# A two-layer decoder on one core: inside a step of the second cross attention, maximum products before score products

## The chip, the cores and the metric

The kernel runs on one core of one Trainium2 chip. The metric is the device time of one execution in microseconds; the time before is the median of three runs. A separate profiled execution gives the rows that are shown here. The engines are called as the profile calls them: PE (TensorE matmul) and PEld (its weight loads), DVE (VectorE), ACT (ScalarE), POOL (GpSimd), and SP, which only issues DMAs.

## The reference, cut to what matters

A decoder of two layers works on 16 batches of 56 tokens and 128 channels. Each layer is a self attention, a cross attention to a context of 1500 positions, and a feed-forward part with experts. The change touches the second layer's cross attention, with 16 heads of 8 channels:

```
def _L1_xattn_ref(q, k, v, W_q, b_q, W_k, b_k, W_v, b_v, W_o, b_o):
    qh = _split_heads(q @ W_q.T + b_q, bs)
    kh = _split_heads(k @ W_k.T + b_k, bs)
    vh = _split_heads(v @ W_v.T + b_v, bs)
    scores = jnp.einsum('bhqd,bhkd->bhqk', qh, kh) / jnp.sqrt(jnp.float32(D_K))
    weight = jax.nn.softmax(scores, axis=-1)
    attn = jnp.einsum('bhqk,bhkd->bhqd', weight, vh)
    concat = attn.transpose(0, 2, 1, 3).reshape(bs, -1, D_MODEL)
    return concat @ W_o.T + b_o
...
x = x + _L1_xattn_ref(_layernorm(x, axis=-1), ctx_1024, ctx_1024, ...)
```

Here q is the normalised token block and k and v are both the context.

## The kernel before

The kernel is written by hand for each engine, with semaphores between them; each engine runs its instructions in the order of the program. The second cross attention is the group of functions whose names begin with `late_`: `late_tensor` (PE), `late_scalar` (ACT), `late_vector` (DVE), `late_gpsimd` (POOL), `late_sync` (SP).

The softmax is done in two passes over the same score matrix. First the row maxima of a batch are found: PE makes a product of queries and keys of 112 rows by 500 columns (`maxima`, L1083), DVE reduces it to one column (L1405), 24 times for a batch. Then the negative maxima are turned by PE (`turn_maxima`, L1091), copied by ACT (L1333), and stored as two more rows of the query tile, a high part and a low part, by two small DMAs that ACT issues (`send_maxima`, L1344). The low part is made by DVE (`low_maxima`, L1420) after DVE's two reductions of that step. With those rows in place a second product gives scores that are already lowered by the maximum (`scores`, L1103: four matmuls, two for each half), ACT takes their exponential straight from PSUM (`exps`, L1324), PE multiplies the result with the values (`product`, L1117: eight matmuls in groups of 32 columns), and POOL adds the exponentials up over the chunks (`add`, L1232) for the row sums, which PE spreads (`sums`, L1125) and DVE inverts (`normalise`). For the last batch DVE does the adding (`last_add`).

The main loop of `rest()` on PE has one step for each chunk c of 125 context positions, 12 steps to a batch, counted by g. In a step with c = g mod 12 of batch b = g div 12, PE does several things that belong to different batches:

- the scores of chunk g - 4 (so that scores lag the maxima by 16 steps);
- two maximum products of batch b + 1;
- in steps c = 2, 3 and 4 a third of the key projection of batch b + 2 (`project`, `keys`, L1042), and in steps c = 6, 8 and 10 a third of its value projection (L1048). All of them use PSUM bank 7, so a third of the keys waits until ACT (L1293, high part) and DVE (L1399, low part) have taken the third before;
- in step c = 0 the turning of the maxima of batch b;
- the product with the values of chunk g - 5;
- in one step of a batch the sums of the batch before.

ACT's loop does in each step the two exponentials first, then the evacuation of the projections, the masked queries of batch b + 2 in step 5 (`queries`, L1311), and the two small DMAs of the maxima in steps 0 and 1. ACT's second small DMA waits for `low_maxima`, and whatever ACT has to do in step 2 stands behind it. DVE's loop does in each step the two reductions and then the rest.

The keys reach the stacked key tile `late_k` by 12 DMAs of 187.5 KB for a batch, issued by SP (`stack`, L1275) as soon as the low part of the last third is ready; the first maximum product of that batch (`maxima` with u = 0, at c = 0) waits for all of them (`m["stack"]`). Maximum products use PSUM banks 0, 1 and 2 in turn, so one waits for the reduction of the third before it (`m["mx"]`). Scores have two banks and wait for the exponential of the same half one step earlier; the exponentials go around five buffers (`LATE_P`).

The lines of the wait for the stack are these:

```
def maxima(b, u):
    ...
    if u == 0:
        pe.wait_ge(m["stack"], 16 * 12 * (b + 1))
```

Of the kernel before, what the change touches and what calls it, by code (L numbers as in the profile page):

```python
# [23 lines left out]
B, S, D = 16, 56, 128  # L24
# [45 lines left out]
def decoder_kernel(nc, t, out):  # L70
# [4 lines left out]
    with ctx:  # L75
# [959 lines left out]
        def late_tensor(pe):  # L1035
            m = la

            def keys(b, piece, bank):

                if piece == 0:  # L1040
                    pe.wait_ge(ld_late[b % 2], 16 * (b // 2 + 1))
                nc.tensor.matmul(PS[:, bank, 0:KB], xa_w[:, 1, :], late_ctx[b % 2][:, piece * KB:(piece + 1) * KB],  # L1042
                                 start=True, stop=True).then_inc(m["kmm"], 1)

            def values(b, piece, bank):
                for j in range(4):
                    c = 4 * piece + j
                    mm = nc.tensor.matmul(PS[0:KC, bank, j * 128:(j + 1) * 128],  # L1048
                                          late_ctx[b % 2][:, c * KC:(c + 1) * KC], xa_w[:, 2, :],
                                          start=True, stop=True)  # L1050
                mm.then_inc(m["vmm"], 1)

            def project(b, piece):

                if piece == 0:
                    if b >= 2:
                        pe.wait_ge(m["nmlow"], b - 1)
                elif piece < 4:
                    pe.wait_ge(m["khi"], 3 * b + piece)
                    pe.wait_ge(m["klo"], 3 * b + piece)  # L1060
                else:
                    pe.wait_ge(m["vev"], 3 * b + piece - 3)
                if piece < 3:
                    keys(b, piece, 7)
                else:
                    values(b, piece - 3, 7)

            def maxima(b, u):

                s, w = u // NKB, u % NKB  # L1070
                if u == 0:
                    pe.wait_ge(m["stack"], 16 * 12 * (b + 1))
                    if b:
                        pe.wait_ge(m["qset"], b)
                if b == 0:
                    if u < NKB:
                        pe.wait_ge(m["qlo"], u + 1)
                    if u % (2 * NKB) == 0:
                        pe.wait_ge(m["q0set"], u // (2 * NKB) + 1)
                if b or s:  # L1080
                    pe.wait_ge(m["mx"], NKB * (8 * b + s - 1) + w + 1)
                at = (s // 2) * S2 + w * KB
                nc.tensor.matmul(PS[0:2 * S, w, 0:KB], late_q[b % 3][0:3 * QUAD, s * 2 * S:(s + 1) * 2 * S],  # L1083
                                 late_k[b % 3][0:3 * QUAD, at:at + KB], start=True, stop=True)\
                    .then_inc(m["mxmm"], 1)

            def turn_maxima(b):

                pe.wait_ge(m["nmsplit"], b + 1)
                pe.wait_ge(m["vev"], 3 * min(b + 2, B))  # L1090
                nc.tensor.transpose(PS[0:8, 7, 0:2 * S], late_nm[b % 2],  # L1091
                                    ident[0:2 * S, 0:2 * S]).then_inc(m["nmtr"], 1)

            def scores(b, c, half):
                at = 2 * (NC * b + c) + half
                if c == 0 and half == 0:
                    pe.wait_ge(m["nmrow"], 2 * 16 * (b + 1))
                if at >= 2:
                    pe.wait_ge(m["exp"], at - 1)
                for a in range(2):  # L1100
                    j = 2 * half + a
                    first = min(j * 4 * S, HQ - SCOLS)
                    mm = nc.tensor.matmul(PS[0:KC, 3 + half, a * SCOLS:(a + 1) * SCOLS],  # L1103
                                          late_k[b % 3][:, j * S2 + c * KC:j * S2 + (c + 1) * KC],
                                          late_q[b % 3][:, first:first + SCOLS], start=True, stop=True)
                mm.then_inc(m["sc"], 1)

            def product(b, c):
                n = NC * b + c
                if c == 0:  # L1110
                    if b >= 2:
                        pe.wait_ge(m["norm"], b - 1)
                    pe.wait_ge(m["vev"], 3 * b + 3)
                pe.wait_ge(m["exp"], 2 * n + 2)
                for j in range(4):
                    r = slice(32 * j, 32 * j + 32)
                    mm = nc.tensor.matmul(PS[r, 5 + b % 2, 0:4 * S], late_v[b % 3][0:KC, c, r],  # L1117
                                          late_p[n % LATE_P][:, j * 4 * S:(j + 1) * 4 * S],
                                          start=c == 0, stop=c == NC - 1)
                mm.then_inc(m["pv"], 1)  # L1120

            def sums(b):
                pe.wait_ge(m["padd"], (NC - 1) * (b + 1))
                for j in range(4):
                    mm = nc.tensor.matmul(PS[32 * j:32 * j + 32, 5 + b % 2, 4 * S:8 * S], ones[0:KC, 0:32],  # L1125
                                          late_acc[b % 2][:, j * 4 * S:(j + 1) * 4 * S], start=True, stop=True)
                mm.then_inc(m["sum"], 1)
# [27 lines left out]
            def rest():  # L1155
                def project_queries(j, a, bank):
                    nc.tensor.matmul(PS[0:3 * QUAD, bank, 0:HALF],
                                     late_wq[:, j, :, :].rearrange("p r c -> p (r c)"),
                                     XN[:, a * HALF:(a + 1) * HALF], start=True, stop=True).then_inc(m["qp"], 1)

                pe.wait_ge(xn_ready, 2 * 4 + 2)
                pe.wait_ge(m["wqrep"], 1)
                for j in range(4):
                    project_queries(j, 0, j)
                for c in range(NC):
                    maxima(0, 2 * c)
                    maxima(0, 2 * c + 1)
                    if c < 3:
                        if c == 0:
                            pe.wait_ge(ld_late[1], 16)  # L1170
                        pe.wait_ge(m["vev"], c + 1)
                        keys(1, c, 4 + c)
                    elif c < 7:
                        if c == 4:
                            pe.wait_ge(m["qlo"], 4)
                        if c > 4:
                            pe.wait_ge(m["klo"], 3 + c - 4)
                        project_queries(c - 3, 1, Q_BANKS[c - 3])
                    elif c < 10:
                        if c == 7:  # L1180
                            pe.wait_ge(m["klo"], 6)
                        else:
                            pe.wait_ge(m["qlo"], c - 3)
                        values(1, c - 7, V_BANKS[c - 7])
                pe.wait_ge(m["qlo"], 8)
                for g in range(NC * B + LAG):
                    b, c = g // NC, g % NC
                    n = g - LAG
                    if 0 <= n:
                        scores(n // NC, n % NC, 0)  # L1190
                        scores(n // NC, n % NC, 1)
                    if b + 1 < B:
                        maxima(b + 1, 2 * c)
                        maxima(b + 1, 2 * c + 1)
                    if b + 2 < B and c in (2, 3, 4):
                        project(b + 2, c - 2)
                    if b + 2 < B and c in (6, 8, 10):
                        project(b + 2, c // 2)
                    if c == 0 and 0 <= b < B:
                        turn_maxima(b)  # L1200
                    if 1 <= n:
                        product((n - 1) // NC, (n - 1) % NC)
                    if n >= NC and n % NC == 2:
                        sums(n // NC - 1)
                    if b == B - 1 and c == 5:
                        pe.wait_ge(m["wo"], 1)
                        out_bias(0, HB)
                        out_heads(0, HB, range(4))
                product(B - 1, NC - 1)
                out_bias(HB, B - 1)  # L1210
                out_heads(HB, B - 1, range(1))
                sums(B - 1)
                out_heads(HB, B - 1, range(1, 4))
                out_bias(B - 1, B)
                out_heads(B - 1, B, range(4))
# [997 lines left out]
```

## Time and profile before

| what | value |
| --- | --- |
| time before, median of three runs | 1419.98 us (1418.58 to 1421.03) |
| profiled execution: span from the first to the last instruction | 1421.9 us |
| profiled execution: its own time, apart from the span | not given separately |
| busy share over the span: PE, PEld, DVE, ACT, POOL | 96%, 71%, 73%, 61%, 54% |
| the steps that hold both score and maximum products, in the span | 902.3 us to 1283 us |
| mean granted TensorE clock over the span | 0.976 of full speed |

The span is that of the one profiled execution; the median is that of other executions. A busy PE is not PE at its peak: matmuls are pipelined and their ends are modelled in the records. A wait for several semaphores is put down to the one that came last.

### The profile page before, as it was taken

Reading aid. Unit: us, or ns where it says so; the run is one execution under the profiler, and the core shown is the slowest. Engines: PE = TensorE matmul, PEld = TensorE weight load, DVE = VectorE, ACT = ScalarE, POOL = GpSimd, SP = SyncE. Lnnn points to the kernel's source line nnn. Section 1 sums busy time; section 2 is a strip of 40 time slices with the busy share of each in tenths; the row PEclk is TensorE's granted clock in tenths of the full one; section 3 lists DMA queues with packets and bytes.
Section 4 is the critical chain, followed back from the end, with each engine's and each line's share of the span. In section 5 each row is a group of like instructions: output and inputs, shape, how many; then the busy total and the mean of one; then the engine's idle time right before and its main releaser. Section 6 shows DMA issues by size and latency. Waiting matters only on the chain.

```text
span 1421.9 us, 25408 instructions
## 1 busy us (share of the span) xinstructions
PE 1361.6 (96%) x9220; PEld 1016.4 (71%) x9220; DVE 1039.0 (73%) x2112; ACT 860.5 (61%) x1849; POOL 766.6 (54%) x431
## 2 busy tenths in 40 slices
PE   7889999999999999999998987899999999999998
PEld 4647888888888888888865754556656556555687
DVE  6458778888777877788854677677777777774687
ACT  4537667666667666677632553466666666664665
POOL 5036443334444444432261292488888888894463
PEclk9899999999999999999998999899999999997999
DMA  3132222211122222221150232535536446330131
GB/s 85 59 94 52 57 58 57 52 39 43 48 54 58 56 53 58 57 57 36 40 156 4 66 67 57 139 88 133 129 89 144 119 99 143 87 96 1 58 107 43
DMA packets 71803, 104.39 MB, mean 73 GB/s; under 512 B 14670, under 2 KB 54934, under 8 KB 71550
## 3 DMA queue, kind: packets, MB, share of 16 engines
q1 hardware_dynamic: 60062, 91.39, 25.8%
q10 hardware_dynamic: 11616, 11.38, 2.8%
q8 instruction: 73, 1.20, 0.4%
q14 instruction: 52, 0.43, 0.1%
HBM read 63.65 MB, written 2.11 MB: 46 GB/s over the span
## 4 chain that ended last, share of the span: by engine, by line
PE 77%; DVE 7%; POOL 4%; ACT 3%; DMA 3%; issue 2%; SPq 1%; ACTq 1%; POOLq 0%; DVEq 0%
PE PS L700 10%; PE PS L714 6%; PE PS L1103 6%; PE PS L688 5%; PE PS L716 5%; PE PS L689 5%; PE PS L715 5%; PE PS L690 5%; PE PS L1117 4%; POOL QO_area L1232 4%; PE PS L1083 3%; PE PS L1042 2%; PE PS L1048 2%; PE PS L1776 2%; PE PS L743 2%
## 5 line engine op out<-in xcount | busy, mean ns | idle before, releaser
L1232 POOL TENSOR_TENSOR QO_area<-QO_area,prob_a 125x896 f32<-125x896 f32 x150 | 315.1, 2101 | 22.7 <-ACT prob_a L1324 3.2
L866 ACT ACTIVATE HL<-PS 125x512 fp32r<-125x512 f32 (+1 forms) x384 | 206.5, 538 | 176.5 <-PE PS L700 161.0
L958 DVE TENSOR_TENSOR HL<-PS,HL 125x512 fp32r<-125x512 f32 (+1 forms) x384 | 238.2, 623 | 73.1 <-ACT HL L866 52.4
L1405 DVE TENSOR_REDUCE QO_area<-PS 112x1 f32<-112x500 f32 x384 | 240.6, 672 | 68.0 <-PE PS L1083 67.8
L1324 ACT ACTIVATE prob_a<-PS 125x448 f32<-125x448 f32 x384 | 187.6, 540 | 111.0 <-PE PS L1103 88.7
L773 POOL TENSOR_TENSOR HL<-ctx_area,ones 125x512 fp32r<-125x512 f32 (+1 forms) x64 | 93.0, 1453 | 244.0 <-PE PS L716 193.9
L1103 PEld LDWEIGHTS PS<-HL 98*125 98x125 f32 x768 | 106.3, 193 | 73.8 <-ACT prob_a L1324 44.8
L688 PE MATMUL PS<-HL 128*128 128x500 f32 x336 | 153.0, 455 | 4.8 <-DVE HL L928 3.9
L714 PE MATMUL PS<-HL 125*128 125x512 f32 (+1 forms) x384 | 155.7, 406 | 1.6 <-DVE HL L958 1.4
L876 ACT ACTIVATE prob_a<-prob_a,neg_max 128x500 f32<-128x500 f32 x192 | 135.5, 706 | 26.7 <-DVE neg_max L950 25.4
L1103 PE MATMUL PS<-HL 98*125 98x256 f32 x768 | 148.6, 317 | 0.6 <-ACT prob_a L1324 0.6
L716 PE MATMUL PS<-HL 125*128 125x512 f32 (+1 forms) x384 | 140.4, 366 | 0.0
L715 PE MATMUL PS<-HL 125*128 125x512 f32 (+1 forms) x384 | 140.1, 365 | 0.0
L1083 PE MATMUL PS<-HL 96*112 96x500 f32 x384 | 126.6, 406 | 6.6 <-DVE QO_area L1405 4.2
L689 PE MATMUL PS<-HL 128*128 128x500 f32 x336 | 131.6, 392 | 0.0
L690 PE MATMUL PS<-HL 128*128 128x500 f32 x336 | 131.1, 390 | 0.0
L700 PEld LDWEIGHTS PS<-ident,prob_a 128*125 128x125 f32 x768 | 113.5, 186 | 17.4 <-ACT prob_a L876 0.9
L776 POOL TENSOR_TENSOR HL<-ctx_area,HL 125x512 fp32r<-125x512 f32 (+1 forms) x64 | 116.7, 1823 | 5.0
L700 PE MATMUL PS<-ident,prob_a 128*125 128x128 f32 x768 | 115.4, 272 | 0.5 <-ACT prob_a L876 0.5
L773 POOL TENSOR_TENSOR HL<-QO_area,ones 128x896 fp32r<-128x896 f32 x15 | 25.2, 1681 | 145.3 <-PE PS L690 130.9
L876 ACT ACTIVATE prob_b<-prob_b,neg_max 128x500 f32<-128x500 f32 x144 | 101.8, 707 | 0.0
L942 DVE CUSTOM_DVE_ANT_0 prob_a<-PS,proj_w,head_scale 128x500 f32<-128x500 f32 x128 | 93.5, 731 | 6.1 <-PE PS L690 1.9
(261 smaller groups left out, 2718.9 us busy)
## 6 DMA issues: line engine op xcount, KB each, us to landing
HL<-prob_b SPq DMA_DIRECT2D x128, 187.5 KB, 4.0
ctx_area<-in_ctx_T SPq DMA_DIRECT2D x16, 750.0 KB, 13.1
ctx_area<-in_ctx SPq DMA_DIRECT2D x16, 750.0 KB
HL<-ctx_area SPq DMA_DIRECT2D x64, 187.5 KB, 3.8
inv_area<-in_ctx_T SPq DMA_DIRECT2D x8, 750.0 KB, 4.1
prob_a<-in_ctx_T SPq DMA_DIRECT2D x8, 750.0 KB, 4.6
inv_area<-inv_kept ACTq DMA_DIRECT2D x16, 256.0 KB, 3.4
ctx_area<-in_L_ffn_W SPq DMA_DIRECT2D x16, 256.0 KB, 3.2
```

Source lines behind the costliest of these rows:

```text
L688: nc.tensor.matmul(dst, qH[b % 2][:, rows], kH[b % 2][:, cols], start=True, stop=False)
L689: nc.tensor.matmul(dst, qH[b % 2][:, rows], kL[b % 2][:, cols], start=False, stop=False)
L700: mm = nc.tensor.transpose(PS[0:KC, 2 + k % 3, j * 128:(j + 1) * 128], tile_prob(GA * g + j)[:, k * KC:(k + 1) * KC], ident[:, :])
L714: nc.tensor.matmul(dst, v_hi, p_hi, start=k == 0, stop=False)
L715: nc.tensor.matmul(dst, v_lo, p_hi, start=False, stop=False)
L716: nc.tensor.matmul(dst, v_hi, p_lo, start=False, stop=k == NC - 1).then_inc(m["pv"], 1)
L866: nc.scalar.activation(pH[k % 3][0:KC, 0:width(g)], PS[0:KC, 2 + k % 3, 0:width(g)], ACT.Copy)\
L876: nc.scalar.activation(p, p, ACT.Exp, bias=neg_max[:, s:s + 1], accum_out=part_sum[:, s, j:j + 1]).then_inc(m["exp"], 1)
L958: nc.vector.tensor_tensor(pL[k % 3][0:KC, 0:width(g)], PS[0:KC, 2 + k % 3, 0:width(g)], pH[k % 3][0:KC, 0:width(g)].bitcast(fp32), ALU.sub ...
L1103: mm = nc.tensor.matmul(PS[0:KC, 3 + half, a * SCOLS:(a + 1) * SCOLS], late_k[b % 3][:, j * S2 + c * KC:j * S2 + (c + 1) * KC], late_q[b % ...
L1232: nc.gpsimd.tensor_tensor(late_acc[b % 2], before, late_p[n % LATE_P], ALU.add).then_inc(m["padd"], 1)
L1405: nc.vector.tensor_reduce(late_part[b % 2][:, u // NKB, u % NKB:u % NKB + 1], PS[0:2 * S, u % NKB, 0:KB], AX, ALU.max).then_inc(m["mx"], 1)
```

## The change

Inside a step of PE's loop the two maximum products are issued ahead of the four score matmuls, not behind them. No instruction is added or taken away; ACT's, DVE's, POOL's and SP's programs stay as they are. In steps without scores (the first four) and without maximum products (batch 15) nothing changes.

```
                 for g in range(NC * B + LAG):
                     b, c = g // NC, g % NC
                     n = g - LAG
+                    if b + 1 < B:
+                        maxima(b + 1, 2 * c)
+                        maxima(b + 1, 2 * c + 1)
                     if 0 <= n:
                         scores(n // NC, n % NC, 0)
                         scores(n // NC, n % NC, 1)
-                    if b + 1 < B:
-                        maxima(b + 1, 2 * c)
-                        maxima(b + 1, 2 * c + 1)
                     if b + 2 < B and c in (2, 3, 4):
                         project(b + 2, c - 2)
```

## Rows read from the trace of the kernel before

**Rows 1.** The page's costliest groups: score matmuls; busy us, mean ns, idle before.

```profile
L1103 PE MATMUL PS<-HL 98*125 98x256 f32 x768 | 148.6, 317 | 0.6 <-ACT prob_a L1324 0.6
```

**Rows 2.** Windows of the changed stage: busy us of each engine, clock, DMA.

```profile
1020.00:1080.00 60.00, 59.25 (x485) 35.74 (x487) 44.39 (x74) 38.28 (x80) 53.37 (x27) 1.00 0.56 134
```

**Rows 3.** Timeline of PE, steps 0 to 3: start, duration, line, operation, count.

```profile
1026.44 0.74 PE L1103 MATMUL PS<-HL 98*125 98x256 f32 x4
...
1028.19 0.74 PE L1103 MATMUL PS<-HL 98*125 98x256 f32 x4
1028.77 0.62 PE L1083 MATMUL PS<-HL 96*112 96x500 f32 x2
1029.32 0.58 PE L1117 MATMUL PS<-prob_a,QO_area 125*32 125x224 f32 x8
1029.84 0.73 PE L1103 MATMUL PS<-HL 98*125 98x256 f32 x4
1030.41 0.62 PE L1083 MATMUL PS<-HL 96*112 96x500 f32 x2
1030.86 1.00 PE L1042 MATMUL PS<-prob_a,proj_w 128*128 128x500 f32 x2
...
1032.31 0.73 PE L1103 MATMUL PS<-HL 98*125 98x256 f32 x4
...
1033.88 1.08 PE L1042 MATMUL PS<-prob_a,proj_w 128*128 128x500 f32 x2 [0.38 <-DVE ctx_area L1399]
```

**Rows 4.** Timeline of ACT in the same steps (ACTq is its DMA issue).

```profile
1026.99 0.98 ACT L1324 ACTIVATE prob_a<-PS 125x448 f32<-125x448 f32 x2 [0.67 <-PE PS L1103]
...
1028.12 0.63 ACTq L1344 DMA_DIRECT2D HL<-QO_area  x1
1028.87 0.98 ACT L1324 ACTIVATE prob_a<-PS 125x448 f32<-125x448 f32 x2 [0.78 <-PE PS L1103]
1030.66 0.63 ACTq L1344 DMA_DIRECT2D HL<-QO_area  x1
1031.41 0.98 ACT L1324 ACTIVATE prob_a<-PS 125x448 f32<-125x448 f32 x2 [1.56 <-DVE QO_area L1420]
1032.28 0.69 ACT L1293 ACTIVATE prob_b<-PS,xa_bias 128x500 fp32r<-128x500 f32 x1
```

**Rows 5.** Timeline of DVE in step 1.

```profile
1029.20 1.26 DVE L1405 TENSOR_REDUCE QO_area<-PS 112x1 f32<-112x500 f32 x2 [0.47 <-PE PS L1083]
1030.38 0.25 DVE L1420 TENSOR_TENSOR QO_area<-PS,QO_area 8x112 fp32r<-8x112 f32 x1
```

**Rows 6.** Waits, 900 to 1260 us: total us, times, longest.

```profile
PE PS L1042 <- DVE ctx_area L1399: 5.5, 14, 0.8
```

**Rows 7.** Last stack DMA of two batches, its landing; PE at two steps 0.

```profile
L1275 SPq DMA_DIRECT2D HL<-ctx_area x1: 945/945/945, 995.8 to 995.8; - x1
...
DMA to landing us min/median/max: 5.0/5.0/5.0
...
L1275 SPq DMA_DIRECT2D HL<-ctx_area x1: 901/901/901, 1022.1 to 1022.1; - x1
...
DMA to landing us min/median/max: 3.8/3.8/3.8
...
922.22 0.71 PE L1083 MATMUL PS<-HL 96*112 96x500 f32 x2 [0.55 <-DMA HL<-ctx_area]
...
1000.21 0.73 PE L1103 MATMUL PS<-HL 98*125 98x256 f32 x4
```

**Rows 8.** Timeline: POOL's first addition of batch 13; PE at batch 14's sums.

```profile
1248.96 2.10 POOL L1232 TENSOR_TENSOR QO_area<-prob_a 125x896 f32<-125x896 f32 x1 [1.53 <-ACT prob_a L1324]
...
1298.12 0.59 PE L1125 MATMUL PS<-QO_area,ones 125*32 125x224 f32 x8 [1.45 <-POOL QO_area L1232]
```

**Rows 9.** Windows after those sums; first matmul of a score block alone.

```profile
1300.00:1317.00 17.00, 17.00 (x105) 9.05 (x105) 12.56 (x13) 9.01 (x18) 0.00 (x0) 0.50 0.00 1
...
1028.19 0.39 PE L1103 MATMUL PS<-HL 98*125 98x256 f32 x1
```

More of the change, by code:

```diff
@@ L1188, in rest @@
                     n = g - LAG
+                    if b + 1 < B:
+                        maxima(b + 1, 2 * c)
+                        maxima(b + 1, 2 * c + 1)
                     if 0 <= n:
@@ L1191, in rest @@
                         scores(n // NC, n % NC, 1)
-                    if b + 1 < B:
-                        maxima(b + 1, 2 * c)
-                        maxima(b + 1, 2 * c + 1)
                     if b + 2 < B and c in (2, 3, 4):
```

## Prediction

> **What bounds the kernel now.** I read the page first, where PE is the busiest engine and its score matmuls hardly ever find it idle (0.6 us in 768) [rows 1]. The windows of the changed stage then show PE busy for 59.25 of 60 us at the full granted clock, 2.4 GHz, with POOL second at 53.37 [rows 2]. So the stage is PE in program order plus what it waits for, and a mere exchange of two blocks that are both needed saves no PE time; only waits can change. The timeline of PE gives the plain step: scores at 1028.19, maxima at 1028.77 (0.58 later), products with the values at 1029.32 (1.13 later), the next scores at 1029.84, so 1.65 us a step [rows 3]. The view of waits shows the one PE wait that returns in each batch: the second third of the key projection waits for DVE's low part of the first (L1399), 14 times for 5.5 us, 0.8 of it once at the start, so about 0.36 each for 13 batches [rows 6]. That counts PE idle after modelled ends. By starts it is larger: in step 2 the projection comes 1.02 after the scores (1029.84 to 1030.86), in step 3 it comes 1.57 after them (1032.31 to 1033.88) [rows 3], so 0.55 is wait.
>
> I followed that wait back. ACT can take the first third only at 1032.28, though PE has it ready at 1031.86, because step 2's two exponentials stand ahead of it, and these begin at 1031.41 because ACT's second small DMA was issued from 1030.66 for 0.63 [rows 3, 4]. That DMA waits for `low_maxima` (1030.38 and 0.25 long), which stands behind DVE's two reductions of step 1 (from 1029.20, 1.26 long), and these follow PE's maxima at 1028.77 by 0.43 [rows 3, 5]. So a wait of PE hangs on where the maxima stand in step 1.
>
> **The change part by part.** No instruction is removed or added.
>
> *Inside a step.* Maxima move from 0.58 to 0. The block behind the products pays for its first weight load: the first score matmul of a block takes 0.39 [rows 9], the mean of all four is 0.317 [rows 1], so the other three take 0.29 and the leader pays 0.10 more. That 0.10 passes to the maxima. So maxima's results come 0.58 - 0.10 = 0.48 earlier in the step; scores start 0.57 later without the 0.10, so that their results come 0.47 later. The new neighbours, maxima then scores then products, are not in the trace. Bounds: 0 if the score weights load behind the maxima, and 0.10 for each of 176 steps, 17.6 us, if they do not. The nearest row is the projection behind the maxima, 0.45 after their start for two products (1030.41 to 1030.86), with no such load showing [rows 3]; I take 0 and leave the upper end out.
>
> *The wait for the keys, in step frame.* Take the steps' starts as they are. Maxima of step 1 at 1028.19, reductions from 1028.72 to 1029.98, `low_maxima` to 1030.23 instead of 1030.63. ACT must be ready by then: exponentials of step 0 begin at 1026.99 + 0.47 = 1027.46, the copy and first small DMA follow as before (1028.12 becomes 1028.57 and ends at 1029.20), those of step 1 start at 1029.32 and leave ACT free at about 1030.2 [rows 4]. So the second DMA goes at 1030.26 for 0.63, exponentials of step 2 start at 1031.01 (their scores would let them start at 1029.84 + 0.55 + 0.47 = 1030.86, where 0.55 is what lies between 1026.44 and 1026.99), 0.40 earlier than 1031.41. The evacuation at 1032.28 would come 0.40 earlier, at 1031.88, but PE's third is ready at 1031.86 with about 0.04 for the signal, so 1031.90 or 0.37 earlier [rows 3, 4]. The low part and PE's next third move with it: 1033.88 becomes 1033.51. What is late next is that evacuation chain itself: the projection could come at 1032.31 + 1.02 = 1033.33, so 0.18 of wait stays. The wait in step 4 is of that kind already and keeps its size. Both sides: at least 0.28 (the DMA 0.1 later than worked out), at most 0.40; I take 0.37. It counts for batches 1 to 13; in batch 0 there are no exponentials yet in steps 2 and 3. 13 x 0.37 = 4.8 us gained.
>
> *The wait for the stacked keys.* The first maximum product of a batch waits for 12 DMAs of SP. It now stands at the start of step 0, and the scores, the turned maxima and the products of the step queue behind it on PE, and ACT's exponentials wait for those scores. Before, the scores ran ahead and covered 0.58. In batch 2 the product waited 0.55 already [rows 7]. For batch 5 the last DMA was issued at 995.8 and landed 5.0 later, at 1000.8: the scores of that step began at 1000.21, so the wait was just covered; now it is open. For batch 6 it landed at 1022.1 + 3.8 = 1025.9 and step 0 began at 1026.44, so half a microsecond stays free [rows 3, 7]. Of the 14 stacks after the first two, batches 2, 5 and 8 have the late landing, eleven do not. A stalled batch loses the score block that no longer runs ahead, 0.57 less the 0.10: 0.47; batch 8's landing is a little earlier, 0.42. Sum 1.4 us lost. Both sides: 0 if landings come 0.5 earlier, 14 x 0.57 = 8 if all come as late as batch 5's. I take what this trace landed, 1.4.
>
> The Trainium skill bears on this place. Its page DMA: Bandwidth & Descriptors, section Anatomy of one DMA, gives a fixed cost of about 2.0 us for a transfer's set-up and completion besides the bytes at 436 GB/s; for 187.5 KB my estimate from it is 2.4 us from issue to landing, and no stack would then be waited for, which makes the sum -4.3. The trace has 3.8 and 5.0 [rows 7], and I go by these.
>
> *The end.* POOL's additions of batches 13 and 14 run without a gap from 1248.96 until PE's sums at 1298.12, for which PE idles 1.45 [rows 8]: there POOL sets the end. Its first addition is released by an exponential [rows 8], and exponentials come 0.47 later in their step: 0.5 us lost, once. In the batches before, POOL idles some 1.5 us ahead of that addition, as in batch 13, so there the 0.47 is covered.
>
> *Other moves, at nothing.* Products wait for the exponentials of the step before: these ended 1.53 after their step's start (1026.44 to 1027.97) and now end at 2.00, 0.35 into the next step, and products stand at 1.13 [rows 3, 4]. That leaves 0.78. Reductions behind `normalise` move with the maxima that wait for them, 0.48 both. SP's loads and its stack wait for DVE's low parts, which don't move against the step.
>
> **Sum.** -4.8 + 1.4 + 0.5 = -2.9 us, from 1421.9 to 1419.0 for the profiled execution, whose own time beside the span isn't known. The median of the runs, 1419.98, lies 1.9 below that span; I carry the difference over: 1417.1.
>
> **The rivals.** A measurement of this kernel tells about 0.2% (2.8 us) from no change.
>
> A, the sum above (chance 0.45). Its bounds, 13 x 0.28 to 13 x 0.40 gained, 0.9 to 2.0 lost to the stack and 0.5 to POOL, give -3.8 to -1.1, so 1416.2 to 1418.9. It straddles the 0.2%.
>
> B, the stack is never waited for, since landings vary (0.15): -4.3, so 1415.7. For it: eleven of 14 were early. Against it: the three late ones are every third batch, which looks like a pattern.
>
> C, ACT takes the place of the wait removed (0.12): scores that come 0.47 later push step 2's exponentials back as far as the DMA brings them forward. Then only the losses stay, +1.9: 1421.9. Against it: by my working the scores are ready 0.15 ahead of ACT.
>
> D, the other side (0.08): the stack is waited for in every batch. It decides from a mean wait of 0.31 a batch (4.8 - 0.5 over 14). With batch 5's 0.57 in all 14 it costs 8.0: +3.7, so 1423.7. The margin of batch 6, half a microsecond, speaks against it.
>
> E, TensorE's clock at the end (0.20). After the 1.45 us of idling the granted clock is 0.50 (1.2 GHz) from about 1300 to 1317 [rows 8, 9]. PE will idle longer there, by the 0.47 at least. If the clock falls a step sooner, one more step runs at the lower level: 105 matmuls in 17.0 us at 12 to a step are 1.94 a step, against 1.65 less the maxima's 0.55, 1.10, at full clock, so 0.84 more: 1417.9 (0.13). If it happens not to fall, DVE, busy for 12.56 of those 17, sets the pace and up to 4.4 come back: 1412.7 (0.07). The Trainium skill, page TensorE: Matmul & The Clock Gate, section on the clock gate, says that the throttled level is the default and that activity releases it, which speaks for the sooner fall.
>
> **How the numbers follow.** The likeliest is A: 1417.1. Faster by over 0.2% is half of A, B, the clock that stays and a little of the clock that falls sooner, 0.23 + 0.15 + 0.07 + 0.03 = 0.48. Slower by over 0.2% is D and the tail of C, 0.10. Within it 0.42. The range for 8 in 10 leaves out D and the clock that stays, and takes in A, B with 1.5 us for its variation, and C: 1414.2 to 1421.9.
>
> **What would show it.** PE's wait for L1399 falls from about 0.36 to near 0 idle in step 3 for 13 batches; `low_maxima` ends 0.40 earlier after the start of step 1; batches 2, 5 and 8 show PE idle some 0.5 ahead of L1083 at step 0; POOL's first addition starts 0.5 later in its step. I am wrong if score weights show at the head of their block, if the stack is waited for in most batches, or if step 2's exponentials wait for scores.

## The result and the profile after

The first comparison put the changed kernel at 1425.47 us (median of 4 executions, 1423.36 to 1429.44) against 1419.28 for the one before: ratio 1.0047, 95% interval 1.0024 to 1.007, so slower by about half a per cent, outside the range that was forecast. A longer comparison later (12 executions, below) gave 1419.83 and a ratio of 0.9998 (0.998 to 1.0017), inside that range. The gain of 2.9 us is in neither. Both are told, since what separates them, TensorE's clock, is part of the answer.

The windows show the whole changed stage, from batch 0's products with the values to the last ones, first of before, then of after. Columns are as in [rows 2]: the stretch, its length, then the busy time of PE, PEld, DVE, ACT and POOL with their instructions, the granted clock, the DMA engines' share and GB/s.

```profile
908.00:1317.00 409.00, 400.95 (x3205) 237.95 (x3204) 291.18 (x462) 255.76 (x535) 346.62 (x165) 0.98 0.45 106
```

```profile
908.70:1319.60 410.90, 403.07 (x3204) 252.68 (x3203) 288.87 (x462) 258.34 (x535) 346.93 (x165) 0.97 0.45 105
```

The stage is 1.9 us longer, its clock lower. The profiled execution's span, 1427.6, is 5.7 above before's 1421.9. The other 3.8 lie ahead of the stage (0.7) and behind it (3.1), where, but for batch 0's first two score steps, the code did not change.

The timeline of PE answers to [rows 3], steps 1 to 4 of a batch that did not wait for its stack:

```profile
1033.09 0.71 PE L1083 MATMUL PS<-HL 96*112 96x500 f32 x2
1033.63 0.64 PE L1103 MATMUL PS<-HL 98*125 98x256 f32 x4
1034.20 0.58 PE L1117 MATMUL PS<-prob_a,QO_area 125*32 125x224 f32 x8
1034.72 0.71 PE L1083 MATMUL PS<-HL 96*112 96x500 f32 x2
1035.27 0.63 PE L1103 MATMUL PS<-HL 98*125 98x256 f32 x4
1035.74 1.00 PE L1042 MATMUL PS<-prob_a,proj_w 128*128 128x500 f32 x2
...
1037.74 0.64 PE L1103 MATMUL PS<-HL 98*125 98x256 f32 x4
1038.37 1.08 PE L1042 MATMUL PS<-prob_a,proj_w 128*128 128x500 f32 x2
```

The second third of the key projection has no idle mark now. It comes 0.63 after the scores, the first one 0.47 after them, so 0.16 of wait is left. The same difference was 0.55 in [rows 3]. A plain step is 1.63 (1033.09 to 1034.72) against 1.65.

The timelines of DVE and ACT in the same steps answer to [rows 4, 5]:

```profile
1034.79 0.25 DVE L1420 TENSOR_TENSOR QO_area<-PS,QO_area 8x112 fp32r<-8x112 f32 x1
```

```profile
1035.07 0.63 ACTq L1344 DMA_DIRECT2D HL<-QO_area  x1
1035.82 0.98 ACT L1324 ACTIVATE prob_a<-PS 125x448 f32<-125x448 f32 x2 [0.61 <-PE PS L1103]
1036.78 0.68 ACT L1293 ACTIVATE prob_b<-PS,xa_bias 128x500 fp32r<-128x500 f32 x1
```

`low_maxima` ends 1.95 after the start of step 1 (1033.09 to 1035.04); in [rows 3, 5] it was 2.44. Step 2's exponentials now wait for the scores, 0.12 behind the DMA's end at 1035.70. That costs nothing, since the evacuation at 1036.78 starts as soon as PE's third ends (1035.74 + 1.00).

The view of waits, 905 to 1320 us, shows what came in return:

```profile
PE PS L1083 <- DMA HL<-ctx_area: 3.9, 4, 1.3
PE PS L1125 <- POOL QO_area L1232: 2.6, 2, 1.8
```

L1399 [rows 6] is gone from the list. The stack's DMAs are waited for four times (batches 2, 5, 8, 13) and not once for 0.55 [rows 7], and PE waits for POOL twice, for 2.6 in all, not once for 1.45 [rows 8]. The first of the four waits, batch 2's, and what the clock did behind it:

```profile
921.57 0.58 PE L1117 MATMUL PS<-prob_a,QO_area 125*32 125x224 f32 x8
923.49 0.82 PE L1083 MATMUL PS<-HL 96*112 96x500 f32 x2 [1.34 <-DMA HL<-ctx_area]
...
925.28 0.98 PE L1117 MATMUL PS<-prob_a,QO_area 125*32 125x224 f32 x8
```

```profile
924.00:934.20 10.20, 10.20 (x46) 5.39 (x46) 4.67 (x8) 3.74 (x8) 7.58 (x4) 0.50 0.02 8
934.20:940.20 6.00, 6.00 (x42) 3.27 (x44) 4.08 (x8) 3.52 (x7) 2.10 (x1) 1.00 0.00 0
...
1020.00:1080.00 60.00, 59.98 (x497) 38.96 (x497) 44.92 (x73) 39.61 (x84) 54.38 (x27) 1.00 0.58 134
```

The step took 3.71 (921.57 to 925.28), and for 10.2 us PE ran at 1.2 GHz: 46 matmuls, for which the next window's rate (42 in 6.0) needs 6.6. So by my estimate 3.6 us went there. The last row answers to [rows 2]: away from these places PE hardly idles, 0.02 in 60 us, in place of 0.75.

The end of the stage answers to [rows 8, 9], POOL's timeline, PE's, and the windows:

```profile
1251.62 2.10 POOL L1232 TENSOR_TENSOR QO_area<-prob_a 125x896 f32<-125x896 f32 x1 [1.12 <-ACT prob_a L1324]
```

```profile
1300.78 0.59 PE L1125 MATMUL PS<-QO_area,ones 125*32 125x224 f32 x8 [1.81 <-POOL QO_area L1232]
```

```profile
1302.80:1323.30 20.50, 20.50 (x116) 10.18 (x114) 12.50 (x13) 9.23 (x18) 3.33 (x4) 0.50 0.00 1
```

From POOL's first addition of batch 13 to PE's sums it is 49.16 us in both kernels (1248.96 to 1298.12, 1251.62 to 1300.78). Whatever PE gains in that stretch becomes wait. Behind it the clock is at half for 20.5 us, before for some 17 [rows 9].

### The profile page after: what moved, and what is told of

The parts are those of the page before. It is cut to its first block, busy times and chain, and to the rows that moved or that the text cites. A ratio compares the mean times of both kernels' runs of the same rounds, so it can differ in the third digit from the quotient of the medians.

```text
span 1427.6 us, 25408 instructions
## 1 busy us (share of the span) xinstructions
PE 1367.5 (96%) x9220; PEld 1034.1 (72%) x9220; DVE 1036.2 (73%) x2112; ACT 863.1 (60%) x1849; POOL 767.0 (54%) x431
## 4 chain that ended last, share of the span: by engine, by line
PE 83%; DVE 6%; SPq 3%; DMA 2%; ACT 2%; POOL 2%; issue 1%; ACTq 0%; POOLq 0%; DVEq 0%
PE PS L700 10%; PE PS L1083 7%; PE PS L714 6%; PE PS L688 5%; PE PS L1117 5%; PE PS L1103 5%; PE PS L716 5%; PE PS L715 5%; PE PS L689 5%; PE PS L690 5%; PE PS L1042 3%; SPq L1275 3%; PE PS L1048 2%; PE PS L1776 2%; PE PS L743 2%; PE PS L1777 2%
## 5 line engine op out<-in xcount | busy, mean ns | idle before, releaser
L1083 PE MATMUL PS<-HL 96*112 96x500 f32 x384 | 145.4, 456 | 9.8 <-DMA HL<-ctx_area 5.3
L1103 PEld LDWEIGHTS PS<-HL 98*125 98x125 f32 x768 | 120.9, 194 | 25.3 <-ACT prob_a L1324 7.5
L1103 PE MATMUL PS<-HL 98*125 98x256 f32 x768 | 130.2, 293 | 0.3 <-ACT prob_a L1324 0.3
L1083 PEld LDWEIGHTS PS<-HL 96*112 96x112 f32 x384 | 55.9, 179 | 85.4 <-issue 48.8
## 6 DMA issues: line engine op xcount, KB each, us to landing
HL<-prob_b SPq DMA_DIRECT2D x128, 187.5 KB, 4.0
HL<-ctx_area SPq DMA_DIRECT2D x64, 187.5 KB, 3.8
```

## Experiments

What each kernel is stands below the table. The median and the ratio to before on the same chip, with its 95% interval; the clock is TensorE's mean granted clock, the median over the executions (before: 0.982 or 0.983 in each comparison but the first, for which it is not on record; 4 executions of the first after, 12 of the others). The ratio is the comparison's own figure and not the quotient of the two medians.

| kernel | us | ratio | clock |
|---|---|---|---|
| after, first | 1425.47 | 1.0047 (1.0024 to 1.007) | 0.973 |
| after again | 1419.83 | 0.9998 (0.998 to 1.0017) | 0.977 |
| step 0 left old | 1420.40 | 0.9995 (0.9972 to 1.0017) | 0.977 |
| step 0 only | 1420.21 | 1.0006 (0.9978 to 1.0034) | 0.982 |
| step 1 only | 1419.44 | 0.9991 (0.9968 to 1.0014) | 0.978 |
| four semaphores | 1417.02 | 0.9977 (0.9954 to 1.0) | 0.978 |
| batch 2's wait filled | 1421.49 | 1.001 (0.9992 to 1.0027) | 0.974 |
| batch 2's step 0 old | 1418.89 | 0.9985 (0.996 to 1.001) | 0.978 |
| code shifted | 1415.96 | 0.9985 (0.9962 to 1.0009) | 0.980 |
| before, four semaphores | 1424.19 | 1.004 (1.0017 to 1.0063) | 0.975 |
| before, late sums | 1419.01 | 0.9999 (0.9975 to 1.0023) | 0.982 |
| after, late sums | 1417.76 | 1.0003 (0.9976 to 1.003) | 0.978 |
| before, both | 1416.77 | 0.9994 (0.9975 to 1.0013) | 0.982 |
| after, both | 1411.26 | 0.9936 (0.9913 to 0.996) | 0.984 |

**Which step carries the gain, which the loss.** Three kernels put the maxima first in some steps only; `first` is `c != 0`, `c == 0` and `c == 1` in turn.

```
+                    first = c != 0
-                    if b + 1 < B:
+                    if b + 1 < B and first:
                         maxima(b + 1, 2 * c)
                         maxima(b + 1, 2 * c + 1)
                     if 0 <= n:
                         scores(n // NC, n % NC, 0)
                         scores(n // NC, n % NC, 1)
+                    if b + 1 < B and not first:
+                        maxima(b + 1, 2 * c)
+                        maxima(b + 1, 2 * c + 1)
```

Step 0 left as it was:

> Maxima first in all steps but step 0 of each batch, where the scores lead as before. Theory 1 (the loss is the wait for the stacked keys at the head of step 0, and the clock that falls in it; elsewhere the new order gains 0.37 at the key projection and about 0.02 in a plain step): steps 0 of batches 2, 5 and 8 wait at most 0.5 us again, the clock stays up at batch 2, step 3 keeps its 2.71 us, and the kernel takes about 1414 us, 5 under before. Theory 2 (the loss is that scores and exponentials come later in each step, down to POOL's last additions and the clock at the end): no better than the changed kernel, 1423 to 1426 us.

Step 0 alone:

> Maxima first in step 0 of each batch only. Theory 1: all of the loss and none of the gain: step 3 keeps 3.08 us, steps 0 of batches 2, 5 and 8 are 0.5 us or more longer than before, with a fallen clock after batch 2's; 1421 to 1427 us. Theory 2: one step in twelve changes little, 1419 to 1420 us.

Step 1 alone:

> Maxima first in step 1 of each batch only, the step whose reductions release ACT's second small DMA. Theory 1: the gain at the key projection alone, 13 x 0.37 = 4.8 us, no new wait at step 0, POOL's first addition where it was: about 1414.5 us, step 3 at 2.71 us. Theory 2: as before, 1419 us.

All three came out even with before. Their waits on the stack, first step 0 left old, then step 0 alone, then step 1 alone:

```profile
PE PS L1083 <- DMA HL<-ctx_area: 0.8, 3, 0.5
```

```profile
PE PS L1083 <- DMA HL<-ctx_area: 1.9, 2, 1.1
```

```profile
PE PS L1083 <- DMA HL<-ctx_area: 0.7, 1, 0.7
```

The 13 waits for the low part of the keys (L1399 in before) are missing from all three lists, with step 0 alone too, where I had expected them to stay. The lengths of the steps, from the starts of their first products in the timelines (medians of batches 1 to 13), tell more. Steps 1 to 3 together take 7.21 us in before, 6.81 in after, 6.80 with step 0 left old, 6.96 with step 1 alone and 7.25 with step 0 alone. So step 1 alone brings 0.25 of the 0.40; with step 0 alone step 3 is 0.26 shorter, but steps 1 and 2 are 0.10 and 0.20 longer, and nothing is won. Step 0 has the loss, as the prediction had it: alone, it waits 1.9 us for the stack; left old, the long waits are gone. Still no time was won with it left old: in that kernel's profile PE waited 2.5 us for POOL in batches 14 and 15, and ran at half clock from 1296.0 to 1319.9. I had expected a clear gain there, and with step 1 alone; the end was not in that working.

**The wait for the stack taken away.** Each quarter of the stack's columns, three DMAs, gets its own semaphore, and a maximum product waits for its quarter alone.

```
+        stack_part = [la["stack"]] + [sem(f"late_stack{j}") for j in range(1, 4)]
...
+                if u % (2 * NKB) == 0:
+                    pe.wait_ge(stack_part[u // (2 * NKB)], 16 * 3 * (b + 1))
...
-                    pe.wait_ge(m["stack"], 16 * 12 * (b + 1))
...
-                                     half[j * QUAD:(j + 1) * QUAD, :].bitcast(fp32)).then_inc(m["stack"], 16)
+                                     half[j * QUAD:(j + 1) * QUAD, :].bitcast(fp32)).then_inc(stack_part[j], 16)
```

> The changed order in all steps, but the 12 DMAs of a stack count on four semaphores, one for each quarter of the columns, and a maximum product waits for the three DMAs of its own quarter only, which land some 5 us after the start where the last lands after 13 to 14. Theory 1: no wait at step 0 in any batch, batch 2's old 0.55 us gone too, the clock stays up at batch 2; 13 x 0.5 gained less 0.5 at POOL's end: about 1412.5 us. Theory 2: as the changed kernel, 1423 to 1426 us.

The waits of this kernel's stage hold no DMA any more, but POOL as before. The windows show the clock nearly full around batch 2, and half behind the sums:

```profile
PE PS L1127 <- POOL QO_area L1234: 2.6, 2, 1.8
```

```profile
908.00:940.00 32.00, 31.68 (x247) 20.00 (x246) 21.84 (x37) 22.11 (x47) 25.37 (x13) 0.98 0.49 113
...
1295.20:1315.70 20.50, 20.50 (x119) 10.99 (x120) 13.78 (x14) 10.09 (x19) 1.20 (x2) 0.50 0.01 2
```

One place of loss is cured, and the ratio, 0.9977, touches 1.

**Is it the wait that lets the clock fall?** The changed kernel again; then with two idle matmuls ahead of batch 2's first maximum product; then with batch 2's step 0 in the old order.

> The changed kernel itself, on the chip of the next three, since executions of one kernel differ by several us. Theory 1 (late landings of the stacked keys at the head of step 0, and the clock that falls at batch 2's): steps 0 of batches 2, 5, 8 and 13 wait again by 0.5 to 1.3 us, and the clock falls at about 924 us; 1421 to 1426 us. If the clock's fall at 924 us was chance, it does not return and the time is about 1421 us.

In this second profile of the changed kernel batch 2's stack alone is waited for; those of batches 5, 8 and 13 are not:

```profile
PE PS L1083 <- DMA HL<-ctx_area: 1.6, 1, 1.6
```

```
+                    if b == 1 and c == 0:
+                        pe.wait_ge(m["vev"], 3 * (b + 2))
+                        hold_clock(2)
```

> The changed kernel with two full matmuls that nobody reads put ahead of batch 2's first maximum product, so that PE works through the 1.3 us in which it waits there (they take about 1.5 us). Theory 1: the clock stays at full speed past 924 us and batch 0's twelve steps shrink from 31.4 to about 28 us, some 3.5 us less in all. Theory 2 (the fall has another cause): the clock falls all the same, and the kernel is as slow as the changed one or 0.2 us slower.

```
+                    first = not (c == 0 and b == 1)
```

> The changed order except in the one step 0 in which batch 2's stacked keys are waited for; there the scores lead as before. Theory 1: that step takes 2.6 us instead of 3.7, no clock falls at 924 us, batch 0's twelve steps take about 26.7 us instead of 31.4, so some 4.7 us less than the changed kernel; batches 5, 8 and 13 still wait. Theory 2: no change against the changed kernel beyond 0.5 us.

Windows behind batch 2's step 0, of the changed kernel again, with the wait filled, and with that step old:

```profile
923.40:933.60 10.20, 10.20 (x46) 5.45 (x45) 4.57 (x8) 3.73 (x8) 7.43 (x4) 0.50 0.02 8
```

```profile
920.00:926.00 6.00, 6.00 (x46) 3.58 (x39) 3.67 (x8) 2.75 (x7) 5.58 (x3) 1.00 0.32 118
926.00:932.00 6.00, 5.97 (x37) 3.05 (x36) 4.22 (x8) 3.94 (x8) 5.57 (x3) 1.00 0.00 1
```

```profile
915.00:925.00 10.00, 9.50 (x79) 5.63 (x77) 6.29 (x12) 6.16 (x13) 9.43 (x5) 1.00 0.48 131
925.00:935.00 10.00, 9.97 (x80) 5.97 (x78) 6.92 (x11) 7.18 (x16) 7.56 (x5) 1.00 0.24 50
```

The clock fell again where PE idled and stayed up where it was kept busy or, with that step old, waited 0.5 us as in before. These are single profiles. In all fifteen kept traces together the clock falls twelve times in this stage, each time behind a wait of PE of 1.3 to 1.8 us; three more such waits have no fall behind them, and the shorter ones (up to 1.1) none at all. But the times did not follow the cure: in both cured kernels' profiles the clock was at half again at the end of the stage, and the filled one came out at 1.001.

**Why the stack is late.** While the stack's last copy is under way, the list of DMA queues holds one packet of 16 KB on the queue for instructions in each late batch, and none in most early ones. I read these packets as fetches of code. The fifteen kept traces have 210 such last copies. The 135 without a packet beside them took 2.8 to 4.1 us from issue to landing; the 40 whose packet began 1.4 to 2.9 us after the issue took 4.5 to 5.9. The 16 whose packet began earlier (from 0.9 us ahead of the issue on) landed by 4.4; of the 19 whose packet began 3.2 us after the issue or later, 14 landed by 4.1 and five at 5.3 to 5.5. In the second profile of after batch 5's packet began 3.3 us after the issue and not 2.3, and the copy landed after 3.8 us and not 5.3. Eleven one-column matmuls at the head of PE's program (44 instructions with their weight loads) shift PE's code against its fetches; the program behind them is the same.

```
+            for i in range(11):
+                nc.tensor.matmul(PS[0:32, 7, 0:1], ident[:, 0:32], ident[:, 0:1], start=True, stop=True)
```

> The changed kernel with 11 one-column matmuls (44 instructions) at PE's very start, so that each of PE's later blocks of code is fetched some 44 instructions (about 2.6 us) earlier against the loop. Theory 1b (a stack's last DMA lands late, at 13.8 to 14.4 us after the stack's start, when a 16 KB code fetch falls 10.5 to 12.3 us after it): the fetches move out of that stretch, every last DMA lands by 13.2 us, no step 0 waits over 0.2 us, and the kernel is 4 to 8 us faster than the changed one. Rival 1c (the late landing belongs to those batches or to their third of the key tile): batches 2, 5 and 8 land late all the same and nothing changes.

Batches 2, 5, 8 and 13 no longer waited; batches 11 and 14 did, where I had expected none to, and batch 11's wait was followed by a clock fall of its own. First the DMA view of after, 918.4 to 923.5 (batch 2's last copy); then of the shifted kernel, 919.7 to 922.7 (batch 2's) and 1149.1 to 1155.1 (batch 11's); then its PE and clock in batch 11, and its clock behind the sums at the end:

```profile
q8 instruction: 1, 0.02, 1.2%
...
HL<-ctx_area SPq DMA_DIRECT2D x1, 187.5 KB, 5.1
```

```profile
q1 hardware_dynamic: 151, 0.60, 93.7%
...
HL<-ctx_area SPq DMA_DIRECT2D x1, 187.5 KB, 3.0
```

```profile
q8 instruction: 1, 0.02, 1.5%
...
HL<-ctx_area SPq DMA_DIRECT2D x1, 187.5 KB, 5.9
```

```profile
1155.06 0.71 PE L1083 MATMUL PS<-HL 96*112 96x500 f32 x2 [1.52 <-DMA HL<-ctx_area]
```

```profile
1157.00:1163.90 6.90, 6.90 (x30) 3.51 (x29) 2.70 (x5) 2.79 (x7) 5.91 (x3) 0.51 0.01 1
1295.00:1312.00 17.00, 14.89 (x141) 7.97 (x139) 13.06 (x13) 11.06 (x21) 2.94 (x2) 1.00 0.01 1
```

The lateness goes with the fetch and not with the batch's number. The traces also have the sixteen increments by which a copy tells of its landing: in each of the 40 copies above fifteen came by 4.3 us and only the last came 0.6 to 2.1 us behind them, while without a packet the last two were at most 0.3 apart. So one part of sixteen is late and not the whole copy.

In the last row of the windows the clock stayed up behind the same 1.8 us wait for POOL. So the fall there is not certain in any one execution, and its price can be read from PE's sums (L1125) to the same later instruction (L1772), in the shifted kernel, in before and in after:

```profile
1298.14 0.59 PE L1125 MATMUL PS<-QO_area,ones 125*32 125x224 f32 x8 [1.80 <-POOL QO_area L1232]
...
1323.72 0.95 PE L1772 MATMUL PS<-gate_w,prob_b 128*56 128x9 f32 x13 [0.74 <-DVE prob_b L390]
```

```profile
1328.81 0.84 PE L1772 MATMUL PS<-gate_w,prob_b 128*56 128x9 f32 x13 [0.74 <-DVE prob_b L390]
```

```profile
1333.23 0.96 PE L1772 MATMUL PS<-gate_w,prob_b 128*56 128x9 f32 x11 [0.74 <-DVE prob_b L390]
```

It is 25.58 us with the clock up, 30.69 in before (from 1298.12 [rows 8]) and 32.45 in after (from 1300.78). The fall cost 5.1 us in before's profile and 6.9 in after's; the change made it 1.8 longer.

**The end set free.** PE's sums of batch 14 move from step 2 to step 6 of batch 15, DVE's division from step 3 to step 7, so that PE does not stand still for POOL there. (It still waits 2.7 to 2.9 us, in the profiles, for DVE's additions of the last batch, behind the stage.)

```
-                    if n >= NC and n % NC == 2:
+                    if n >= NC and n % NC == (6 if n // NC == B - 1 else 2):
                         sums(n // NC - 1)
...
-                    if n >= NC and n % NC == 3:
+                    if n >= NC and n % NC == (7 if n // NC == B - 1 else 3):
                         normalise(n // NC - 1)
```

With the two cures and the two orders there are eight kernels. Before and after are two of them, after with four semaphores a third. The other five, first the old order with the semaphores alone:

> The order of before, with the stack's twelve copies counted on four semaphores, one for each quarter of its columns, so that a maximum product waits for its own three copies alone. The new order gained .5 us a batch in every run so far; if the order is the source and the finer wait only takes the stack's waits away, this kernel gains nothing but batch 2's wait of before at step 0 (about .5 us): plain batch 26.15 as before, no step 0 above 1.9, time .999 to 1.001 of before. If the finer wait was itself the gain seen with the new order and four semaphores (.9977), this one shows it too: 1416 to 1417. End of the stage as before: PE's wait for POOL in batch 14 about 1.5 us, and the half-speed stretch there in few executions, mean clock .981 or so.

The new order with both cures:

> The new order with the four semaphores, and in the last batch PE's sums of the batch before move from step 2 to step 6 and VectorE's division from step 3 to step 7. Theory 1, PE reaches those sums 3 us before POOL has finished its additions, idles, and the clock then falls to half in most executions and costs some 6.5 us: the 3 us wait goes, the clock stays up there, batch 15's twelve steps take 20 us and not 27, and most executions have a mean clock of .981 or more: 1411 to 1414, .994 to .997 of before. Theory 2, the stage's end is bound by POOL's additions wherever PE stands: the wait comes back in batch 15, at its own sums, the clock falls there or not as before, and the time is that of the four-semaphore kernel, 1416 to 1418. Theory 3, the clock falls at the end of the stage without a wait ahead of it: no PE wait over 1 us, clock still .50 for 15 to 20 us after 1295.

The old order with the late sums alone:

> The order of before, with the sums of batch 14 moved from step 2 to step 6 and the division from step 3 to step 7, and nothing else. Theory 1, the end's wait and the clock behind it are before's own cost too, only rarer (wait 1.45 us): the wait goes, the clock stays up in nearly all executions; 1415 to 1417.5, .997 to .999 of before. Theory 2, additions bound the end anyway: 1419. If this kernel and the new order with the same move differ by 5 us or more, the new order's .5 us a batch reaches the end once the end is free; if they differ by less than 2, the order is worth little even then.

The new order with the late sums alone:

> The changed kernel with batch 14's sums moved from step 2 to step 6 and the division from step 3 to step 7, and one semaphore for the stack as it was changed. Theory 1, the loss has two places that add up, the stack's waits at step 0 (with the clock's fall behind batch 2's) and the wait for POOL in the last batch (with the fall there): the second alone is gone here, so the time lies between the changed kernel's 1420 and the 1411.3 of the kernel with both cured: 1414 to 1417; batch 2's step 0 still 3.5 to 4 us, the clock falling behind it for about 10 us, the clock up after 1290. Theory 2, the end is the only place that counts: 1411 to 1413. Theory 3, the end counts for nothing without the finer wait: 1419 to 1421.

The old order with both:

> The order of before with both cures: four semaphores for the stack, and the sums and the division of batch 14 four steps later. It differs from the fastest kernel so far (1411.3) in the order alone. Theory 1, the order is worth .5 us a batch where nothing takes it back, 13 batches and batch 13's .9 less 1.0 in batch 14: 1417.5 to 1418.5, with plain batches of 26.15 against 25.65 and equal rows in batch 15. Theory 2, the fastest kernel owes its time to the two cures and not to the order: 1411 to 1413. Theory 3, an execution's time is mostly the chance of where the clock falls early in the program and the order is lost in it: anywhere from 1412 to 1420, with a mean clock that differs from the .984 of the fastest kernel and accounts for the difference.

The whole stage and its end in the windows, first the new order with both cures, then the old order with both:

```profile
906.30:1300.80 394.50, 392.06 (x3205) 247.93 (x3204) 284.55 (x458) 257.66 (x535) 346.90 (x165) 1.00 0.47 109
1282.60:1300.80 18.20, 17.89 (x156) 9.67 (x155) 10.11 (x10) 11.39 (x23) 6.92 (x4) 1.00 0.01 1
```

```profile
907.70:1308.00 400.30, 393.85 (x3205) 234.60 (x3204) 287.13 (x458) 255.20 (x535) 346.64 (x165) 1.00 0.46 108
1290.00:1308.00 18.00, 17.69 (x156) 9.60 (x155) 10.30 (x10) 11.35 (x23) 6.52 (x4) 1.00 0.01 1
```

These two differ in the order alone, at full clock throughout the stage and with like ends: 5.8 us in the stage, and 5.5 between the medians (of two comparisons on two chips; 7.0 when each is taken from its own before, 1418.79 and 1417.34). Of the 5.8, 4.0 is PE's idle time (400.30 - 393.85 = 6.45 against 394.50 - 392.06 = 2.44), the other 1.8 are in the blocks themselves. The old order gains nothing measurable from either cure or both. The new order gains clearly only with both. With late sums alone it still waits for the stack:

```profile
PE PS L1083 <- DMA HL<-ctx_area: 3.7, 4, 1.3
```

```profile
915.48 0.70 PE L1083 MATMUL PS<-HL 96*112 96x500 f32 x2 [1.28 <-DMA HL<-ctx_area]
```

That is one profiled execution in which the clock stayed up behind batch 2's wait; its stage was 398.6 us, 4.1 more than with both cures. Its twelve executions reach from 1411.73 to 1425.59, and their median is just above the 1414 to 1417 that I had expected.

I had expected the late sums to help the old order, and they did not. And one result I cannot place: the old order with four semaphores at 1.004. Its steps are those of before and no step 0 waits; in its profile the clock was at half from 1291.3 to 1311.8, and its mean clock is 0.975. I know no cause in its own edit.

## Why the prediction was wrong

*The wait for the keys* was right in place and size. Taken 0.37 a batch; step 3's wait went from 0.55 to 0.16, 0.39, and 0.18 had been said to stay. `low_maxima` ends 0.49 earlier, not 0.40. Step 1, to which I had put all of it down, brings 0.25 when it is changed alone.

*The block's first weight load* was right, and more came of it. Means of the two kinds in 1020 to 1080 us of after:

```profile
L1083 PE MATMUL PS<-HL 96*112 96x500 f32 x56 | 19.8, 435 | 0.0
L1103 PE MATMUL PS<-HL 98*125 98x256 f32 x112 | 17.8, 281 | 0.0
```

In before the same view has 390 and 307. Four scores less 26 ns each are 0.10, two maxima plus 45 are 0.09: the load passes to the maxima and the upper end of 17.6 us is out. A plain step is 0.02 shorter, which I had at 0.

*The wait for the stacked keys* is the first term that failed. I took 1.4 us for three batches by the landings of one execution. After's first profile has four waits of 3.9 us together, against 0.55 before; its second has one of 1.6. In the first, batches 2, 5 and 8 were the right ones, but batch 5's last copy landed 5.3 after its issue and not 5.0, and batch 8's 5.4; batch 13, not among them, waited 0.5. The landings are no property of the batch: they change with where a code fetch falls, also from one execution to the next, and my "0 if landings come 0.5 earlier" should have had an "or later by as much" beside it, for any batch. The Trainium skill, page DMA: Bandwidth & Descriptors, section Queues, rings and completion order, says that each DMA engine takes turns between queues and finishes a whole packet before it goes to the next. The trace agrees as far as it goes: a 16 KB packet held one engine for about 1.0 us (1.2% of 16 engines in 5.1 us), and of a late copy one part in sixteen is late. That this part stood behind the packet, on the same engine, is argued: the traces do not name the engine. My estimate from that page, 2.4 us, lies below every landing here (2.6 at least); the section it was taken from describes DMAs that GpSimd issues, and SP issues these.

*What a stalled PE costs* was the second and the larger miss. I priced a stalled batch by its idle time alone and let the clock fall only at the end. It fell behind batch 2's wait in both profiles of the changed kernel, some 3.6 us each. Rival E had the mechanism and neither the place nor the size: at the end before's profile had a fall already, of 5.1 us, and the change made it 1.8 longer where I had 0.84; a clock that stays up there is worth 5.1 and not 4.4.

*The end.* POOL's first addition of batch 13 came 0.45 later in its step; I had 0.5. The steps' first products, in before and in after:

```profile
1247.37 0.73 PE L1103 MATMUL PS<-HL 98*125 98x256 f32 x4
```

```profile
1249.58 0.71 PE L1083 MATMUL PS<-HL 96*112 96x500 f32 x2
```

The addition follows 1.59 behind the one (1248.96) and 2.04 behind the other (1251.62). Not seen was the consequence for PE: the sooner it is there, the longer it stands (1.45 to 2.6 in two waits). That more executions then have the clock at half behind it is read from the mean clocks alone and not shown: 0.973 and 0.977 in the median for after against 0.982, where 17 us at half speed are 0.006 of the mean. The four kernels of the new order or part of it whose waits at the end are 2.4 us or more, and whose sums are not moved, have 0.974 to 0.978, the shifted one 0.980. The old order with the semaphores alone, 1.5 us of wait and 0.975, does not fit that row. With late sums and the stack cured it is 0.984 and the time comes.

*The rivals.* B failed, the stack is waited for. C's condition came about and cost nothing. D is out: ten of 14 stacks were not waited for in after's first profile, 13 in its second. A, the sum, fell by its second term and by the clock that it left out. So -2.9 became about nothing to +0.5%: the 5.8 us that the order is worth were given back at batch 2, in one profile at three more stacks, at the wait for POOL and to the clock.

*What stays open.* How the loss divides over executions: one trace is kept of each kernel (two of the changed one), so where the clock fell in the others is not known, only its mean. Why the first four executions were all at 0.973 and the next twelve were not, and why the semaphores alone slowed the old order, isn't settled either. At 0.4%, a difference between two kernels here may be the clock and not the edit; the stage's windows tell them apart.

## What to carry to other kernels

A wait that is removed moves the engine forward everywhere, also up to the next thing that is late: look ahead of time for what the engine will meet sooner, here the stacked keys and POOL's additions, and cure these in the same change; alone, the order, the semaphores and the late sums gained nothing measurable (the semaphores lost 0.4%), together they gained 0.64% (0.40 to 0.87). Where twelve transfers share one semaphore, the first user waits for the last of them; a semaphore for each part that is used at a time makes the landing of the last one harmless. And price a stall of TensorE by what its clock may do behind it, not by its idle time alone.

## What the runs showed of the hardware

- The last copy of a stack, 187.5 KB within the core, took 2.8 to 4.1 us from issue to landing without a code fetch beside it (135 copies in fifteen traces), and 4.5 to 5.9 with one that began 1.4 to 2.9 us after its issue (40 copies), by one part in sixteen; shifting PE's code by eleven matmuls moved the late landings to other batches.
- TensorE's clock fell to half 0.5 us after a wait of 1.34, for 10.2 us, though PE was busy for the whole of them; and behind a wait of 1.28 in another kernel it did not. In the fifteen traces it fell behind 12 of 15 waits of 1.28 to 1.82 in this stage, and behind no shorter one. The Trainium skill, page TensorE: Matmul & The Clock Gate, section What's actually happening, says that the chip's look at PE's activity runs freely and isn't started by the kernel. The runs fit that, without showing the look itself: like waits are followed by a fall in some executions and not in others.
- Which of two blocks pays for a weight load is seen in the mean durations, and here it went to the block behind the products: 0.10 us passed from the scores to the maxima.
